# Weights of layers 1 to 3 loaded, turned and folded inside the first group, of a four-layer attention kernel

## The reference, cut to what matters

```python
def reference(x, ctx, mask, mask2, ...):
    # layer 0: attention over the 256 columns, 64x64 weights
    Mn = Wn @ inorm(x) + bn;  Mm = Wm @ inorm(ctx) + bm;  Ml = Wl @ ctx + bl
    A = softmax(Mn.T @ Mm);   x = Wo @ (Ml @ A.T) + bo + x
    # layer 1: 32 query heads of 8 on 8 key heads, keys and values from ctx
    q, k, v = x @ Wq + bq, ctx @ Wk + bk, ctx @ Wv + bv
    x = layernorm(attend(q, k, v, mask) @ Wo + bo + x) * gamma + beta
    # layer 2: 16 heads of 16, queries from x, keys and values from [ctx; x], then an MLP 256-1024-256
    out = attend(x @ q_w + q_b, [ctx; x] @ kv_w + kv_b, mask2) @ out_w + out_b + x
    x = gelu(rmsnorm(out) * post @ mlp_w1 + b1) @ mlp_w2 + b2 + x
    # layer 3: a recurrent block; its weights are applied turned
    xa = ln(x); sx = shifted(xa) - xa
    xxx = tanh((xa + sx * maa_x) @ maa_w1) @ maa_w2
    xk, xw, xv, xr, xg = xa + sx * (maa_stack + xxx)
    w = exp(-exp(decay + tanh(xw @ td_w1) @ td_w2))
    r, k, v, g = xr @ Wr.T, xk @ Wk.T, xv @ Wv.T, silu(xg @ Wg.T)
    # state s per head: out = r.(u*k*v + s);  s = k*v + w*s, over the 64 rows
    x1 = x + groupnorm(out) * g @ Wo.T
    return x1 + sigmoid(xr2 @ Wfr.T) * (relu(xk2 @ Wfk.T)**2 @ Wfv.T)
```

## Time and profile before

| | us |
|---|---|
| median of 3 runs | 2005.09 (2001.06 to 2007.68) |
| the profiled execution | 2005.4 |
| its span in the trace | 2003.3 |

### The profile page before, as it was taken

One profiled execution on the slowest core, in us unless ns is written; L12 is line 12 of the kernel. 1 busy time (PEld: TensorE's weight loads), 2 busy tenths in 40 slices (PEclk: granted clock), 3 DMA queues, 4 the chain that ended last, 5 costly groups with the idle time before them and its releaser, 6 DMA issues.

```text
span 2003.3 us, 36727 instructions
## 1 busy us (share of the span) xinstructions
PE 1673.5 (84%) x13614; PEld 1033.5 (52%) x13614; DVE 1275.2 (64%) x2181; ACT 931.7 (47%) x1831; POOL 801.7 (40%) x894
## 2 busy tenths in 40 slices
PE   3788898898988899798988989888987989888825
PEld 2465555564564645555555655546455555556203
DVE  3453468844796557854688457965589546883383
ACT  1555544545545444546445455454545454453202
POOL 3542137603474036611376024840367114760070
PEclk9899899999999999999989989999999999899757
DMA  6001005110241004210041102420042101410070
GB/s 175 1 2 35 1 7 59 24 41 4 29 49 38 18 1 54 34 27 18 10 56 23 38 7 25 52 39 18 1 55 34 27 18 14 52 24 12 0 85 11
DMA packets 73584, 60.92 MB, mean 30 GB/s; under 512 B 38961, under 2 KB 56513, under 8 KB 73409
## 3 DMA queue, kind: packets, MB, share of 16 engines
q1 hardware_dynamic: 49600, 41.70, 16.6%
q10 hardware_dynamic: 23264, 16.85, 3.0%
q0 software_dynamic: 544, 0.03, 0.0%
HBM read 20.28 MB, written 4.19 MB: 12 GB/s over the span
## 4 chain that ended last, share of the span: by engine, by line
PE 56%; ACT 15%; DVE 11%; issue 7%; POOL 6%; DMA 2%; ACTq 0%; DVEq 0%; POOLq 0%; SPq 0%
PE bank L680 24%; PE bank L819 6%; PE bank L1017 6%; PE bank L696 3%; PE bank L914 3%; PE bank L960 3%; ACT soft_ring L1156 3%; POOL soft_ring L1618 3%; DMA late<-late 2%; DVE late L1316 2%; PE bank L985 2%; PE bank L759 2%; ACT soft_ring L1175 2%; DVE soft_ring L1463 2%; ACT late L1047 2%
## 5 line engine op out<-in xcount | busy, mean ns | idle before, releaser
L1618 POOL TENSOR_TENSOR soft_ring<-soft_ring,seg_max 128x512 f32<-128x512 f32 x256 | 276.7, 1096 | 273.2 <-DVE seg_max L1469 272.5
L1175 ACT ACTIVATE soft_ring<-soft_ring 128x512 f32<-128x512 f32 x256 | 160.6, 627 | 228.5 <-POOL soft_ring L1618 216.0
L1580 POOL TENSOR_TENSOR late<-late 128x520 f32<-128x520 f32 x128 | 189.0, 1477 | 156.4 <-DMA late<-late 118.9
L1316 DVE TENSOR_TENSOR_SCAN late<-late 128x520 f32<-128x520 f32 x128 | 218.5, 1707 | 22.0 <-DVE xr L1494 6.7
L960 PE MATMUL bank<-ident,soft_ring 128*128 128x128 f32 x1024 | 170.0, 295 | 51.1 <-ACT soft_ring L1175 46.3
L1463 DVE SCALAR_TENSOR_TENSOR soft_ring<-bank,mask 128x512 f32<-128x512 f32 x256 | 164.2, 682 | 34.8 <-PE bank L819 25.7
L960 PEld LDWEIGHTS bank<-ident,soft_ring 128*128 128x128 f32 x1024 | 116.4, 147 | 135.0 <-ACT soft_ring L1175 83.7
L1469 DVE TENSOR_REDUCE seg_max<-soft_ring 128x8 f32<-128x512 f32 (+1 forms) x256 | 166.2, 675 | 6.2 <-DVE early L1527 2.0
L1626 POOL TENSOR_SCALAR soft_ring<-soft_ring,rden 128x256 f32<-128x256 f32 x64 | 61.6, 962 | 265.4 <-DVE rden L1436 265.4
L819 PE MATMUL bank<-early 64*128 64x512 f32 (+1 forms) x512 | 120.3, 556 | 56.4 <-ACTq L1159 53.6
L1047 ACT ACTIVATE late<-bank 128x512 f32<-128x512 f32 (+2 forms) x104 | 62.0, 596 | 204.4 <-PE bank L680 200.3
(11 more groups left out here) (246 smaller groups left out, 3357.6 us busy)
## 6 DMA issues: line engine op xcount, KB each, us to landing
late<-late SPq DMA_DIRECT2D x128, 260.0 KB, 4.4
c<-in_ctx ACTq DMA_DIRECT2D x8, 512.0 KB, 4.2
x<-in_x ACTq DMA_DIRECT2D x8, 512.0 KB, 5.2
out_x<-late SPq DMA_DIRECT2D x8, 512.0 KB, 2.9
mask<-in_mask_Bx1xSxS_ff ACTq DMA_DIRECT2D x16, 128.0 KB, 4.5
w<-in_L_xattn_mlp_w ACTq DMA_DIRECT2D x2, 1024.0 KB
mask<-in_mask_BxS_ik SPq DMA_DIRECT2D x8, 256.0 KB, 3.5
wkv<-in_L_xattn_kv_w ACTq DMA_DIRECT2D x1, 512.0 KB
```

Source lines behind the costliest of these rows:

```text
L1175: af(soft[:, u % SOFT, :], soft[:, u % SOFT, :], ACT.Exp).then_inc(sig("exp"), 1)
L1316: nc.vector.tensor_tensor_scan(sj[:, n % 2, :], wP[:, k, :, :].rearrange("p b t -> p (b t)"), aj[:, n % 2, :], 0.0, ALU.mult, ALU.add).the ...
L1580: tt(aj[:, n % 2, :], kP[:, k, :, :].rearrange("p b t -> p (b t)"), vj[:, n % 3, :], ALU.mult).then_inc(sig("kv_done"), 1)
L1618: tt(s, s, seg_max[:, u % SOFT, 0:segs].unsqueeze(2).broadcast_to([128, segs, 512 // segs]), ALU.subtract).then_inc(sig("sub"), 1)
```

## The change

The prologue keeps what layer 0 of group 0 needs: the inputs, the first mask, the four weights of layer 0, the bias rows of layers 0 and 1, the identity, the band masks. All else moves into program 0.

- SP issues the weights, in the order of their use, at the head of program 0 (`load_weights`), POOL its 17 rows (`load_rows`).
- PE and DVE have a function `prepare(i)` that is called at the head of each iteration of program 0: the product of the value bias with layer 1's output weights at iteration 9, the rows' turn at 16, the same product for layer 2 at 20, and the eight square weights at 23, 25, ... 37 on PE, each copied back by DVE at the next even iteration.
- They take their banks from the ring `late`, and the unturned weights and rows lie in the buffer `late`, both without use in program 0.
- Waits on the loads are added where each weight is first used.
- In the prologue ACT issues the second input right behind the first, then two of layer 0's weights, then the masks; POOL makes the identity first; DVE normalises the inputs ahead of its copies and masks.

```diff
-        vrows = early[:, 10240:10368]
+        vrows = late[:, 2048:2176]
+        wo_by_lane = cut(late, 2560, KT, E)
+        staged = {w: cut(late, 4096 + 512 * n, KT, E) for n, w in enumerate(SQUARE)}
...
-                load_ahead(act, 0, lambda: None, lambda: None)
+                act.dma_start(c0[:, :, :], c_in[0]).then_inc(sig("c0_in"), 16)
+                act.dma_start(x0[:, :, :], x_in[0]).then_inc(sig("x0_in"), 16)
+                act.wait_ge(sig("zeroed"), 1)
+                for w in ("Wm", "Wn"):
+                    for h in range(2):
+                        act.dma_start(conv[w][64 * h:64 * h + 64, 64 * h:64 * h + 64], a[f"L0_xattn_{w}"]).then_inc(sig("conv_in"), 16)
+                for rows in (slice(0, 64), slice(64, 128)):
+                    act.dma_start(mask1[rows, :, :], mask1_in[0]).then_inc(sig("mask1_in"), 16)
                 nc.scalar.preload_act_table_set(LOG_EXP)
...
-                    act.dma_start(cut(early, 512 * n, KT, E), a[f"L3_xattn_{w}"].rearrange("(k p) n -> p k n", p=128)).then_inc(sig("square_in"), 16)
...
                 deviations_ahead(act, link, 1)
...
-                pe.wait_ge(sig("bands"), 1)
-                pe.wait_ge(sig("rows_all"), 1)
+                pe.wait_ge(sig("ident_made"), 1)
                 pe.wait_ge(sig("conv_in"), 128)
                 t, full = fill(pe, "turn", "conv")
                 for n, w in enumerate(conv):
                     ins = nc.tensor.transpose(t[:, 128 * n:128 * n + 128], conv[w][:, :], ident[:, :])
                 ins.then_inc(full, 1)
...
-                pe.wait_ge(sig("square_in"), 16 * len(SQUARE))
-                for n, w in enumerate(SQUARE):
...
+            def load_weights(sp):
+                for t, name in ((staged_wq.rearrange("p k h g d -> p k (h g d)"), "L1_xattn_Wq"), (wk1[:, :, :], "L1_xattn_Wk"), (wv1[:, :, :], "L1_xattn_Wv")):
+                    sp.dma_start(t, rows(name)).then_inc(sig("l1_in"), 16)
...
+                for t, name in ((wkv2, "L2_xattn_kv_w"), (wq2, "L2_xattn_q_w"), (wo2, "L2_xattn_out_w")):
+                    sp.dma_start(t[:, :, :], rows(name)).then_inc(sig("l2_in"), 16)
...
+                for w in SQUARE:
+                    sp.dma_start(staged[w], rows(f"L3_xattn_{w}")).then_inc(sig("square_in"), 16)
...
+                def prepare(i):
+                    if i == 9:
+                        pe.wait_ge(sig("wo1_in"), 16 * 16)
+                        pe.wait_ge(sig("bias_spread"), 1)
+                        t, full = fill(pe, "late", "row1")
+                        for g in range(2):
+                            ins = mm(t[:, 0:E], spread[:, 0, :], wo1[:, g, :], start=g == 0, stop=g == 1)
+                        ins.then_inc(full, 1)
+                    if i == 16:
+                        pe.wait_ge(sig("more_rows_in"), 16 * 2)
+                        pe.wait_ge(sig("pool_rows_in"), 16 * (15 + 2))
+                        t, full = fill(pe, "late", "vec")
+                        tr(t[:, 0:128], vrows, ident[:, :])
+                        pe.wait_ge(sig("lane_rows"), 1)
+                        tr(t[:, 128:256], vrows_by_lane, ident[:, :]).then_inc(full, 1)
...
+                    for n, w in enumerate(SQUARE):
+                        if i == 23 + 2 * n:
+                            pe.wait_ge(sig("square_in"), 16 * len(SQUARE))
+                            t, full = fill(pe, "late", w)
+                            src = staged[w]
...
                 for i in range(END):
                     step()
+                    if before is None:
+                        prepare(i)
                     layer0(i)
...
+                if before is None:
+                    pe.wait_ge(sig("mlp_in"), 16 * 2)
+                    pe.wait_ge(sig("mix_in"), 16 * (2 + NMIX + 1))
...
+                def prepare(i):
...
+                    if i == 10:
+                        dve.wait_ge(sig("spread_in"), 16 * 5)
+                        t, free = take(dve, "row1")
+                        link(tt(row1[:, :], t[:, 0:E], row1[:, :], ALU.add))
+                        dve.sem_inc(free, 1)
+                        dve.sem_inc(sig("row1_ready"), 1)
+                    if i == 16 - 1:
+                        dve.wait_ge(sig("more_rows_in"), 16 * 2)
+                        dve.wait_ge(sig("pool_rows_in"), 16 * (15 + 2))
...
+                    if i == 20 + 1:
+                        t, free = take(dve, "row2")
+                        link(tt(row2[:, :], t[:, 0:E], row2[:, :], ALU.add))
+                        dve.sem_inc(free, 1)
+                        link(tt(row2[:, :], row2[:, :], spread_beta, ALU.add))
+                        tt(row_b2[:, :], row_b2[:, :], spread_beta, ALU.add).then_inc(sig("rows_ready"), 1)
+                    if i == 23 - 2:
+                        dve.wait_ge(sig("square_in"), 16 * len(SQUARE))
+                        for o in range(KT):
+                            for m in range(KT):
+                                at = slice(128 * m, 128 * m + 128)
+                                ins = nc.vector.tensor_copy(wo_by_lane[:, o, at].rearrange("p (c e h) -> p c e h", c=4, e=2),
+                                                            by_lane(staged["Wo"][:, o, at]))
+                        ins.then_inc(sig("lane_wo"), 1)
+                    for n, w in enumerate(SQUARE):
+                        if i == 23 + 2 * n + 1:
+                            t, free = take(dve, w)
...
+                            else:
+                                nc.vector.tensor_copy(wt[w][:, :, :].rearrange("p k n -> p (k n)"), t[:, :]).then_inc(free, 1)
...
+                if before is None:
+                    load_rows(pool)
```

270 lines of the change are left out of this document (131 added, 139 removed).

## The result

| | before | changed |
|---|---|---|
| median of 4 runs each, us | 2004.84 (2001.06 to 2007.68) | 1985.72 (1984.37 to 1987.32) |
| the profiled execution | 2005.4 | 1985.88 |
| its span | 2003.3 | 1984.2 |

The ratio is 0.9903, 95% interval 0.9889 to 0.9916: the changed kernel is 1% faster, by 19.1 us. The forecast was 1989.6 us.

The account below looks back on a forecast made before the run. TensorE (PE, busy 84%) was taken to set the pace, behind a 42.1 us prologue. Start 26.9 us earlier less costs of 11.4 gives 15.5, so 1989.6 us; its own range 1984 to 1995, with rivals and scatter 1982 to 1997.

Parts of the forecast that it names:

- start of group 0: End of the prologue: group 0 starts near 15.2 instead of 42.12, 26.9 us earlier, bounds 22 to 27.6.
- cold clock: Group 0's first products: TensorE starts at 1.2 GHz and they warm it, costing 2.9 us, bounds 0 and 7.4.
- POOL's issues: Group 0's head: POOL's 17 loads, 8.95 us, just fit before its first own work, costing 0.
- to iteration 13: Group 0 up to iteration 13: row 1's bias product and DVE's small pieces fall in waits, costing 0.3 us, bounds 0 and 1.7.
- iterations 15 to 17: PE waits for DVE's copy of the rows, scores of units 2 and 3 behind it: 1.4 us, bounds 0.3 and 2.
- first attention: Units 4 to 15: row 2, four weight turns and DVE's copies on saturated PE cost 4.4 us, bounds 3.4 and 8.9.
- between and after, to the MLP: Between the attentions and after: turns of Wfk and Wfr 1.2, DVE's copies of Wfr and Wfv 1.2; 2.4 us, bounds 0 and 5.
- input chain: Prologue, from ACT's issue of x: landing 6.6, subtractions to 12.2, copies, `vec` columns and small masks done at 14.2.
- rows' chain: Prologue, SP's issues end at 9.7, bv lands 3 us later at 12.7, turn, copy and masks done at 14.5.
- third rival: POOL's 17 load issues held up by DVE's work, POOL 11 us late: net 5, 2000 us; chance 0.04.
- The fourth: Slower: all weights on one queue land too late for DVE at iteration 21, 2006 us and more; chance 0.02.
- first rival: Absorbed: turns and copies fill waits, group 0 pays only 2.9 clock and 3.4 PE; net 20.6, 1984.5 us; chance 0.17.

Follow-up runs that it names:

- first pair: First profiles of the kernel before and the changed kernel: group 1 started 13.7 us earlier, the span ended 19.1 us earlier.
- second profile: The changed kernel profiled and timed again with no edit, against the kernel before: 1986.72 us, ratio 0.9902.
- second pair: Both kernels profiled again with no edit: changed against before, 16.6 us earlier at group 1's start and 9.8 at the end.
- fillers: Changed kernel plus 32 turns of the identity on PE in the prologue and 8 behind the rows' turn: 1983.18 us; with squares at iterations 52 to 59 too, 1985.11.
- third kernel with fillers: Changed kernel with identity turns, the rows' copy by lane at iteration 13 and the squares at iterations 52 to 59 together: 1984.72 us, ratio 0.9888.

## Why the prediction was right, and which terms were off

Right: the sign, the mechanism, and the place of gain and costs. The range held the time, which is 3.9 us below the point. The net of the first pair comes out within 0.5 us of the forecast, but partly by luck, since the errors of the terms cancel.

| term | forecast | measured |
|---|---|---|
| start of group 0 | 26.9 earlier | 27.8 |
| cold clock | 2.9 | 1.7, second profile 2.4 |
| POOL's issues | 0 | 0 |
| to iteration 13 | 0.3 | 0.4 |
| iterations 15 to 17 | 1.4 | 2.5, of it 1.6 clock |
| first attention | 4.4 | 3.7 |
| between and after, to the MLP | 2.4 | 4.5, of it 2.4 clock |
| net at the MLP | 15.5 | 15.0, second pair 17.1 |

*Start.* The input chain came out as worked: statistics of x at 6.76 (6.6), subtractions ended at 12.2 (12.2), last tile 13.6 (14.2). The rows' chain was 1.4 faster: `bv` landed 1.2 us after its issue ended, where I took 3. The run with ACT's new order alone bears out that DVE's standing still had held the start by 2.3 us at most; the rest was SP's chain and the turns and copies behind it.

*Clock.* The term exists: 5.40 us for the first eight products against 3.67, and the first four in 1.96 again with fillers. In this execution the first record of 2.4 GHz is 3.5 us into the work, not 5.8. In the five others with the same head and no fillers it is 3.9, 4.8, 5.3, 5.8 and 6.0 us into it, and the price goes up to 3.0. So the forecast of 2.9 lies inside what was seen, near its top, and 1.7 is the lowest of six. The Trainium skill, page "TensorE: Matmul & The Clock Gate", Part 1, calls the throttled state the default that activity releases; the cold products, and that they went with the fillers in two kernels, agree. The third kernel with fillers (3.75 us) shows a limit: there the clock had fallen again at 13.3, ahead of the group.

*POOL.* 0.52 apiece and 1.95 us of waiting behind them refute the third rival. The fourth is refuted too: the squares landed 33 us before they were needed.

*Iterations 15 to 17.* PE waited 2.05 us for the rows' copy by lane, against 1.55 that it had waited there before; the copy took 0.62 us, where I had 0.3 and where it took 0.28 in the run that has it earlier. The larger part, 1.6, is a fall of the clock right behind this wait. Seven executions have this wait of 2.05 us, and six of them have the fall; neither kernel with the earlier copy has it. The seventh, with the fillers alone, has the wait and no fall, so the fall goes with the wait, but that the wait causes it isn't shown.

*First attention.* PE was busy 26.15 of 30.70 us against 22.92 of 27.00 in the same stretch before: 3.2 us more, for 3.4 forecast, and 0.5 more idle, for 1.0. PE wasn't saturated over the whole stretch: the 15.00 of 15.00 us were its dense middle, and the stretch before had 4.1 us of PE's idle time and 7.6 of DVE's. That sum hides which pieces paid: the squares 2.0, the `vec` pieces on DVE 1.0, row 2's product nothing; 0.8 I can't place. DVE's three additions of row 2 and beta stand in it too, and no run took them away alone.

*Between and after.* The stretches with the turns of Wfk, Wfr and Wfv lost 0.4 and 1.7 us. I had 1.2 for turns and 1.2 for DVE's copies ahead of reductions, 2.4 in all, and 2.1 came. The copies of Wfr and Wfv lie inside the stretch of 24.39:

```profile
114.05 0.69 DVE L1583 COPY t_Wfr<-bank 128x512 f32<-128x512 f32 x1 [0.24 <-DVE early L1472]
...
119.47 0.69 DVE L1583 COPY t_Wfv<-bank 128x512 f32<-128x512 f32 x1
```

How the 1.7 us divide between turns and copies isn't shown. The 41.36 against 41.37 us to the MLP say nothing of them, since the last copy ends at 120.2. What isn't in the forecast is 2.4 of clock.

By kinds, then, 7.1 us of work were lost where 8.5 were forecast, and 5.7 of clock where 2.9 were; the start was 0.9 better. The three errors nearly cancelled. In the second pair group 0 lost 10.9 us (28.0 less 17.1); with the same 7.1 of work that leaves 3.8 of clock, an estimate. So the clock's part isn't a fixed price of the change.

Of the signs that I gave, two don't hold to the letter: PE wasn't busy all the time in the first attention, and POOL's first scaling came 11.4 us after the group's start, not within 10, without a cost that the rows show. The first product, at 14.34, is just ahead of the 14.5 to 17 that I named.

The first rival (absorbed, 1984.5) is nearer to the median than the forecast is, but not in mechanism: where it pays 3.4 us of work, 7.1 were paid. The forecast sum doesn't account for the whole gain of the median. The medians differ by 19.1 and 18.0, the two pairs of profiles by 15.2 on average at group 1. Behind group 1 nothing in the profiles favours the change: three executions of the old layout took 1780.7 to 1786.9 (mean 1783.5), nine of the new 1779.8 to 1790.0 (mean 1783.8). The 3 to 4 us between stay open. Two profiles of each kernel, which differ by 4.4 and 1.4 at group 1 and up to 7.5 in their spans, are too few to place them.

## What to carry to other kernels

Work moved out of a prologue is paid where it lands, and the price is read from a stretch of the clock's full rate between two products that both kernels have; there it repeats to 0.02 us, while whole times scatter by 10 and more. An engine that stands still in a prologue is no gain in itself: ask which chain ends last. Put displaced turns where their engine waits for something else (about 2 to 3 us against 4.2 here), and don't judge a wait's removal by its own rows: of that of the rows' copy, 0.85 us was given back at the next mask.
